# Products of ones on the tensor engine before x arrives, a power in two halves, and another order of work in the first block of an attention and feed-forward kernel

## The reference

```python
xn = _layernorm(x, axis=-1)
x = x + attn(xn, qkv_w, qkv_norm_w, proj_w, proj_norm_w, norm_w, s) + ffn(xn, w_gate, w_up, w_down)
# attn: h = rmsnorm(xn) * qkv_norm_w; q, k, v = h @ ternary(qkv_w).T, 16 heads of 32
#       per chunk of 128 tokens: (q k^T * decay mask) v + (q * decay) S, with a running state S
#       two rmsnorms of the result, then @ ternary(proj_w).T
# ffn:  (silu(xn @ w_gate.T) * (xn @ w_up.T)) @ w_down.T, 2048 hidden features
# ternary(w): w over its mean absolute value, rounded and clipped to -1, 0, 1
```

## Time and profile before

| | |
|---|---|
| median of 3 runs | 1362.63 us (1362.43 to 1362.7) |
| the profiled execution's own time | 1361.45 us |
| its span | 1359.7 us |
| granted TensorE clock, mean of the span | 1.000 |
| busy: PE, DVE, ACT, POOL | 98%, 68%, 36%, 5% of the span |

### The profile page before, as it was taken

One profiled execution on the slowest core, in us unless ns is written; L12 is line 12 of the kernel. 1 busy time (PEld: TensorE's weight loads), 2 busy tenths in 40 slices (PEclk: granted clock), 3 DMA queues, 4 the chain that ended last, 5 costly groups with the idle time before them and its releaser, 6 DMA issues.

```text
span 1359.7 us, 21928 instructions
## 1 busy us (share of the span) xinstructions
PE 1334.2 (98%) x8332; PEld 721.3 (53%) x8332; DVE 924.6 (68%) x1886; ACT 486.5 (36%) x915; POOL 67.5 (5%) x88
## 2 busy tenths in 40 slices
PE   5899999999999999999999999999999999999999
PEld 3455555555455554555545555555545555455554
DVE  6988995576655766657766677657775576755655
ACT  7964633233233332333323233223332233232331
POOL 5600000000000000000000000000000000000000
DMA  8242234113431145211351113510145112431121
GB/s 314 83 142 67 87 73 120 26 32 67 111 88 28 30 79 124 53 32 40 71 140 35 29 40 70 148 40 26 38 85 132 32 30 49 94 94 32 32 48 47
DMA packets 193767, 98.72 MB, mean 73 GB/s; under 512 B 127104, under 2 KB 179328, under 8 KB 192000
## 3 DMA queue, kind: packets, MB, share of 16 engines
q1 hardware_dynamic: 193376, 97.30, 28.3%
q10 hardware_dynamic: 288, 0.01, 0.0%
HBM read 34.35 MB, written 8.39 MB: 31 GB/s over the span
## 4 chain that ended last, share of the span: by engine, by line
PE 94%; DVE 3%; ACT 1%; DMA 1%; SPq 1%; issue 1%; POOL 0%; DVEq 0%; POOLq 0%
PE bank L517 89%; PE bank L559 2%; PE bank L586 1%; PE bank L588 1%; DVE wg_lo L1292 0%; SPq L935 0%; DMA xin<-x 0%; ACT wg_lo L1142 0%; DMA k_stack<-k_parts 0%; DVE arena L861 0%; DMA q_stack<-q_parts 0%; DVE arena L747 0%; DVE xt L748 0%; DVE wd_lo L1292 0%; DVE wu_lo L1292 0%
## 5 line engine op out<-in xcount | busy, mean ns | idle before, releaser
L517 PE MATMUL bank<-wd_hi,arena 128*128 128x512 f16 x1024 | 317.0, 379 | 0.0
L517 PE MATMUL bank<-xt,wg_hi 128*128 128x512 f16 x1024 | 306.5, 381 | 3.6 <-ACT ql L728 1.6
L517 PE MATMUL bank<-xt,wu_hi 128*128 128x512 f16 x1024 | 304.6, 379 | 0.0
L517 PE MATMUL bank<-xt,wg_lo 128*128 128x512 f16 x512 | 195.0, 381 | 0.0
L517 PE MATMUL bank<-wd_lo,arena 128*128 128x512 f16 x512 | 194.0, 379 | 0.0
L517 PE MATMUL bank<-xt,wu_lo 128*128 128x512 f16 x512 | 194.0, 379 | 0.0
L517 PEld LDWEIGHTS bank<-wd_hi,arena 128*128 128x128 f16 x1024 | 100.2, 98 | 115.3
L789 DVE TENSOR_TENSOR sm<-bank,mask 128x512 f32<-128x512 f32 x128 | 88.1, 688 | 105.4 <-PE bank L559 105.3
L517 PEld LDWEIGHTS bank<-xt,wu_hi 128*128 128x128 f16 x1024 | 99.0, 98 | 104.4 <-issue 0.5
L517 PEld LDWEIGHTS bank<-xt,wg_hi 128*128 128x128 f16 x1024 | 98.2, 98 | 103.5 <-issue 4.6
L673 ACT ACTIVATE sm_hi<-sm 128x512 f16<-128x512 f32 x128 | 80.1, 626 | 193.5 <-DVE sm L789 193.5
(11 more groups left out here) (200 smaller groups left out, 1492.2 us busy)
## 6 DMA issues: line engine op xcount, KB each, us to landing
k_stack<-k_parts SPq DMA_DIRECT2D x192, 64.0 KB, 2.2
q_stack<-q_parts SPq DMA_DIRECT2D x192, 64.0 KB, 2.2
arena<-x SPq DMA_DIRECT2D x8, 1024.0 KB, 5.9
out<-arena SPq DMA_DIRECT2D x32, 256.0 KB, 2.4
xin<-x SPq DMA_DIRECT2D x30, 256.0 KB, 4.5
stage<-up_t SPq DMA_DIRECT2D x4, 1024.0 KB, 5.3
stage<-down_t SPq DMA_DIRECT2D x4, 1024.0 KB, 4.9
stage<-gate_t SPq DMA_DIRECT2D x3, 1024.0 KB, 4.8
```

Of the source, the lines that this page charges most:

```text
L517: last = e.matmul(dst, a, b, start=start and n == 0, stop=stop and n == len(lhs) - 1)
```

## The change

On the PE, ahead of the first list, come 30 products of 128x128 by 128x512, written to the bank of SC, which nothing else uses then; they read the part of the transposed x that is filled later, set to ones by one DVE memset. Eight follow that memset, four follow the arrival of each of the four tiles of x, and six follow the first half of the variances. Nothing reads their result.

DVE announces the variance for the layer norm (var_0 part 0) as soon as it is written and that for the rms norm (part 1) later; POOL takes the power of each with an instruction of its own, where it took one over both. HX waits for the second.

The order lists of the first block are new for all engines. Every item is still there. Only the changed lines of the lists' beginnings and ends are shown.

```diff
@@ FIRST_ORDER: the lists of the first block, to where it needs Q, K and V, and their ends @@
     "PE": [
-        ('WT', 0), ('FX', 0), ('FX', 1), ('FX', 2), ('FX', 3), ('WT', 1), ('G', 0), ('U', 0), ('G', 1), ('U', 1), ('G', 2),
-        ('SO', 0), ('FT', 0), ('WT', 2), ('FT', 1), ('WT', 3), ('U', 2), ('G', 3), ('U', 3), ('FT', 2), ('G', 4), ('SO', 1),
-        ('U', 4), ('G', 5), ('WT', 4), ('FT', 3), ('U', 5), ('WT', 5), ('G', 6), ('U', 6), ('K', 0), ('Q', 0), ('V', 0),
-        ('V', 1), ('SC', 0, 0), ('KT', 0), ('G', 7), ('O', 0, 0), ('OX', 0, 0), ('SC', 0, 1), ('Q', 1), ('K', 1), ('KV', 0),
...
-        ('SC', 7, 1), ('G', 15), ('OX', 7, 0), ('KV', 7), ('O', 7, 1), ('U', 15), ('OX', 7, 1), ('D', 2, 2), ('D', 2, 3),
-        ('D', 3, 0), ('D', 3, 1), ('D', 3, 2), ('ZT', 2), ('ZT', 3), ('D', 3, 3), ('PJ', 2), ('PJ', 3),
+        ('WT', 0), ('FX', 0), ('FX', 1), ('FX', 2), ('FX', 3), ('WT', 1), ('G', 0), ('U', 0), ('G', 1), ('WT', 2), ('U', 1),
+        ('G', 2), ('U', 2), ('WT', 3), ('FT', 0), ('FT', 1), ('FT', 2), ('G', 3), ('U', 3), ('G', 4), ('SO', 0), ('WT', 4),
+        ('U', 4), ('G', 5), ('U', 5), ('G', 6), ('SO', 1), ('WT', 5), ('U', 6), ('FT', 3), ('K', 0), ('Q', 0), ('V', 0),
+        ('V', 1), ('G', 7), ('SC', 0, 0), ('KT', 0), ('D', 0, 0), ('O', 0, 0), ('OX', 0, 0), ('SC', 0, 1), ('K', 1),
...
+        ('SC', 7, 1), ('G', 15), ('U', 15), ('OX', 7, 0), ('KV', 7), ('O', 7, 1), ('PJ', 1), ('OX', 7, 1), ('D', 2, 2),
+        ('D', 2, 3), ('D', 3, 0), ('D', 3, 1), ('ZT', 2), ('ZT', 3), ('D', 3, 2), ('D', 3, 3), ('PJ', 2), ('PJ', 3),
...
     "ACT": [
-        ('WA', 0), ('WA', 1), ('WH', 0, 0), ('FX', 0), ('FX', 1), ('FX', 2), ('FX', 3), ('SA', 0), ('SA', 1), ('SA', 2),
-        ('WH', 0, 1), ('WH', 0, 2), ('WH', 1, 0), ('WH', 0, 3), ('WH', 1, 1), ('G', 0), ('SA', 3), ('WH', 1, 2), ('SA', 4),
-        ('WH', 1, 3), ('UH', 0), ('SA', 5), ('G', 1), ('WA', 2), ('WA', 3), ('UH', 1), ('FT', 0), ('G', 2), ('WH', 2, 0),
-        ('WH', 2, 1), ('WH', 3, 0), ('WH', 3, 1), ('FT', 1), ('G', 3), ('SA', 6), ('UH', 2), ('UH', 3), ('FT', 2), ('WA', 4),
-        ('G', 4), ('EL', 0), ('EM', 0), ('WA', 5), ('G', 5), ('UH', 4), ('UM', 0), ('UM', 1), ('UM', 2), ('UM', 3),
-        ('UM', 4), ('UM', 5), ('UH', 5), ('FT', 3), ('K', 0), ('G', 6), ('Q', 0), ('WH', 4, 0), ('WH', 4, 1), ('WH', 5, 0),
-        ('WH', 5, 1), ('V', 0), ('V', 1), ('UH', 6), ('SC', 0, 0), ('KT', 0), ('UM', 6), ('Q', 1), ('SC', 0, 1), ('K', 1),
...
+        ('WA', 0), ('WA', 1), ('FX', 0), ('WH', 0, 0), ('FX', 1), ('FX', 2), ('FX', 3), ('WH', 0, 1), ('WH', 0, 2),
+        ('WA', 2), ('WH', 1, 0), ('WH', 0, 3), ('WH', 1, 1), ('G', 0), ('WH', 1, 2), ('SA', 0), ('SA', 1), ('SA', 2),
+        ('G', 1), ('UH', 0), ('SA', 3), ('SA', 4), ('SA', 5), ('WA', 3), ('WH', 1, 3), ('G', 2), ('WH', 2, 0), ('UH', 1),
+        ('SA', 6), ('G', 3), ('WH', 2, 1), ('WH', 3, 0), ('FT', 0), ('FT', 1), ('UH', 2), ('UH', 3), ('WA', 4), ('WH', 3, 1),
+        ('G', 4), ('FT', 2), ('EL', 0), ('EM', 0), ('G', 5), ('WA', 5), ('UM', 0), ('UM', 1), ('UM', 2), ('UM', 3),
+        ('UM', 4), ('UM', 5), ('FT', 3), ('UH', 4), ('UH', 5), ('K', 0), ('G', 6), ('Q', 0), ('WH', 4, 0), ('WH', 4, 1),
+        ('WH', 5, 0), ('V', 0), ('UH', 6), ('WH', 5, 1), ('V', 1), ('SC', 0, 0), ('KT', 0), ('UM', 6), ('K', 1),
...
     "DVE": [
         ('S4', 0), ('N4', 0), ('WT', 0), ('WC', 0, 0), ('FX', 0), ('FX', 1), ('FX', 2), ('FX', 3), ('WT', 1), ('WC', 0, 1),
-        ('WC', 1, 0), ('WC', 1, 1), ('WC', 0, 2), ('WC', 0, 3), ('U', 0), ('QN', 0), ('HX', 0), ('WC', 1, 2), ('WC', 1, 3),
-        ('UL', 0), ('SS', 0), ('U', 1), ('HX', 1), ('HX', 2), ('HX', 3), ('SO', 0), ('WT', 2), ('WT', 3), ('FT', 0),
-        ('UL', 1), ('U', 2), ('WC', 2, 0), ('WC', 2, 1), ('WC', 3, 0), ('FT', 1), ('U', 3), ('WC', 3, 1), ('UL', 2),
-        ('UL', 3), ('RD', 0), ('SO', 1), ('FT', 2), ('U', 4), ('RD', 1), ('WT', 4), ('U', 5), ('HD', 0), ('WT', 5),
-        ('UL', 4), ('WN', 0), ('UL', 5), ('FT', 3), ('K', 0), ('U', 6), ('Q', 0), ('WC', 4, 0), ('WC', 4, 1), ('WC', 5, 0),
-        ('SC', 0, 0), ('V', 0), ('WC', 5, 1), ('SL', 0, 0), ('KT', 0), ('V', 1), ('SC', 0, 1), ('Q', 1), ('SL', 0, 1),
...
+        ('WC', 1, 0), ('WC', 1, 1), ('WC', 0, 2), ('QN', 0), ('WC', 0, 3), ('U', 0), ('WC', 1, 2), ('HX', 0), ('HX', 1),
+        ('HX', 2), ('HX', 3), ('WT', 2), ('U', 1), ('UL', 0), ('WT', 3), ('SS', 0), ('U', 2), ('WC', 1, 3), ('UL', 1),
+        ('WC', 2, 0), ('U', 3), ('WC', 2, 1), ('WC', 3, 0), ('FT', 0), ('SO', 0), ('FT', 1), ('UL', 2), ('WC', 3, 1),
+        ('FT', 2), ('UL', 3), ('U', 4), ('RD', 0), ('RD', 1), ('U', 5), ('WT', 4), ('SO', 1), ('HD', 0), ('WT', 5),
+        ('WN', 0), ('FT', 3), ('UL', 4), ('UL', 5), ('K', 0), ('U', 6), ('Q', 0), ('WC', 4, 0), ('WC', 4, 1), ('WC', 5, 0),
+        ('V', 0), ('SC', 0, 0), ('WC', 5, 1), ('SL', 0, 0), ('KT', 0), ('V', 1), ('D', 0, 0), ('SC', 0, 1), ('KV', 0),
...
+        ('D', 2, 2), ('NA', 3), ('D', 2, 3), ('NR', 1), ('ST', 1), ('NZ', 1), ('D', 3, 0), ('XN', 1), ('D', 3, 1), ('TX', 2),
+        ('TX', 3), ('TH', 2), ('ZT', 2), ('D', 3, 2), ('ZT', 3), ('D', 3, 3), ('TH', 3), ('PJ', 2), ('PJ', 3),
...
     "POOL": [
-        ('S4', 0), ('RD', 2), ('RD', 3), ('RD', 4), ('RD', 5), ('RD', 6), ('MS', 0), ('NR', 0), ('ST', 0), ('NR', 1),
+        ('S4', 0), ('RD', 2), ('RD', 3), ('RD', 4), ('MS', 0), ('RD', 5), ('RD', 6), ('NR', 0), ('ST', 0), ('NR', 1),
         ('ST', 1),
...
     "SP": [
-        ('WL', 3), ('WL', 4), ('WL', 5), ('YL', 0), ('K', 0), ('Q', 0), ('WL', 6), ('WL', 7), ('V', 0), ('Q', 1), ('K', 1),
-        ('Q', 2), ('K', 2), ('WL', 8), ('Q', 3), ('K', 3), ('Q', 4), ('K', 4), ('Q', 5), ('K', 5), ('WL', 9), ('WL', 10),
-        ('K', 6), ('Q', 6), ('WL', 11), ('Q', 7), ('K', 7), ('TH', 0), ('TH', 1), ('XT', 0), ('TX', 2), ('TX', 3), ('TH', 2),
+        ('WL', 3), ('WL', 4), ('WL', 5), ('YL', 0), ('K', 0), ('Q', 0), ('WL', 6), ('WL', 7), ('V', 0), ('K', 1), ('Q', 1),
+        ('Q', 2), ('K', 2), ('WL', 8), ('K', 3), ('Q', 3), ('Q', 4), ('K', 4), ('WL', 9), ('WL', 10), ('Q', 5), ('K', 5),
+        ('WL', 11), ('K', 6), ('Q', 6), ('K', 7), ('Q', 7), ('TH', 0), ('TH', 1), ('XT', 0), ('TX', 2), ('TX', 3), ('TH', 2),
@@ -398,6 +399,7 @@
         "pro_chain", "beta_sum", "ternary", "piece_max", "piece_scale",
         "beta_total", "beta_part", "clipped"))
     s_inverse, s_clip_pool, s_total = sem("beta_inverse"), sem("clipped_pool"), sem("beta_read")
+    s_warm = sem("warm_tile")
     s_spread, s_allmax = sem("piece_max_spread"), sem("piece_max_read")
     s_var0, s_rs0 = sem("first_variance"), sem("first_scale")
     s_whi, s_wlo = ([sem(f"piece_{k}{n}") for n in range(2)] for k in ("hi", "lo"))
@@ -1067,9 +1069,9 @@
             def first_item(it):
                 kind, n = it[:2]
                 if kind == "S4":
-                    e.wait_ge(s_var0, 1)
-                    e.tensor_tensor(rs_0, var_0[:, 0:2, :], mhalf_0.rearrange("p (a c) -> p a c", a=2), ALU.pow)\
-                        .then_inc(s_rs0, 1)
+                    for k in range(2):
+                        e.wait_ge(s_var0, k + 1)
+                        e.tensor_tensor(rs_0[:, k, :], var_0[:, k, :], mhalf_0[:, 0:TPB], ALU.pow).then_inc(s_rs0, 1)
                     for j in range(GROUPS):
                         e.tensor_scalar(lam_q[:, j, :], ramp, part[:, 0, j:j + 1], part[:, 1, j:j + 1], ALU.mult, ALU.add)
                         last = e.tensor_scalar(lam_k[:, j, :], ramp_back, part[:, 0, j:j + 1], part[:, 2, j:j + 1],
@@ -1151,6 +1153,19 @@
         @block.tensor
         def _(e):
             e.sem_inc(pe["ZT"].sem, pe["ZT"].before)
+            e.wait_ge(s_warm, 1)
+
+            def keep_busy(n):
+
+                for _ in range(n):
+                    e.matmul(b_sc[:, :], xt[0][:, 0, 0:P], xt[0][:, 0, :], start=True, stop=True)
+
+            keep_busy(8)
+            for c in range(TPB):
+                e.wait_ge(ld_first[c], 16)
+                keep_busy(4)
+            e.wait_ge(s_var0, 1)
+            keep_busy(6)
             e.wait_ge(s_ident, 3)
             def first_item(it):
                 kind, n = it
@@ -1190,6 +1205,7 @@
                 ins.then_inc(s_pro, 1)
                 e.wait_ge(s_pro, done[0])
 
+            e.memset(xt[0][:, 0, :], 1.0).then_inc(s_warm, 1)
             e.memset(state1[:, :], 1.0)
             e.wait_ge(s_ident, 3)
             link(e.tensor_reduce(pm4[:, :], ident[:, :].rearrange("p (d h) -> p h d", h=HPG), axis=AX.X, op=ALU.add))
@@ -1214,7 +1230,8 @@
                     for c in range(TPB):
                         last = e.bn_aggr(mv_0[:, c, :], st6_0[:, c, :])
                     link(last)
-                    link(e.tensor_scalar(var_0[:, 0, :], mv_0[:, :, 1], LN_EPS, None, ALU.add))
+                    e.tensor_scalar(var_0[:, 0, :], mv_0[:, :, 1], LN_EPS, None, ALU.add).then_inc(s_var0, 1)
+                    e.wait_ge(s_var0, 1)
                     link(e.reciprocal(var_0[:, 2, :], var_0[:, 0, :]))
```

(1 more changed line is left out.)

## The result

The changed kernel takes 1366.13 us, the median of 8 runs (1365.6 to 1367.95), beside 1362.51 for the kernel before (8 runs, 1361.9 to 1362.94): ratio 1.0029, 95% interval 1.0018 to 1.004. It is 3.6 us slower, just outside the predicted range. Its profiled execution took 1365.87 us with a span of 1364.1, 4.4 us more than the span before. Busy shares are as they were (PE 98%, DVE 68%); the mean granted clock is 0.996 where it was 1.000.

The account below looks back on a forecast made before the run. Three engines together were taken to limit the first block to about 80 us, the PE everything from about 85. Losses of 8.2 us against 8.8 made 0.6 less, median 1362.63 to 1362.0, range 1357.0 to 1366.0.

Parts of the forecast that it names:

- Rival 3: At the first G: the clock has fallen again and the products are in vain, 1363.0 us; chance 0.18.
- the wait for QN: First block: DVE's U(0) stands behind QN, whose transfer lands at 25.0 us; PE waits 1.3 us at U(1).
- the sum: PE idle time in the new order, added from 19 to 80 us: 7.8 us, and 0.2 for the start.
- the sum's end at 80 us: At O(0,0), 77.7 to 79.4 us with D(0,0) already done: PE between 0.8 us ahead and 0.9 behind.
- Does the clock hold?: Nearly idle 4.9 us ahead of G(0): a fallen clock costs 2.5 us, 1.5 hidden, 1363.0 instead of 1362.0; left undecided.
- Rival 2: POOL's MS ahead of RD(5) delays K(0), decided by K(0) past 64.5: 3.4 us more, 1365.4, or 1366.3; chance 0.23.
- Rival 1: The new order closes the waits at WT(4), G(6), U(6), K(0) and O(0,0): 4.5 us less, 1357.5; chance 0.36.

Follow-up runs that it names:

- after_bridge: The changed kernel with 33 more products of 256 columns in the PE's gap ahead of the first G: 1365.6 us, 1.0018 to the kernel before.
- fix1: The changed kernel with SO(0) put back early on PE and DVE, POOL's order still new: 1364.26 us, 1.0012 to the kernel before.
- hyb_old_mspool: Old order up to K(0), new behind it, products and halved power, with POOL's MS ahead of RD(5) and RD(6): 1364.29 us, 1.0008 to the kernel before.
- after_pool2: The changed kernel with WN behind V(1), POOL's RD(5) ahead of MS, and HD behind UL(5) on DVE: 1366.1 us, 1.0026 to the kernel before.
- fix4: The changed kernel with SO(0) and SO(1) early and POOL's old order, RD(5) and RD(6) ahead of MS: 1365.97 us, 1.002 to the kernel before.
- after_again: The changed kernel unaltered, run and profiled a second time beside the two mixed orders: 1366.67 us, 1.0025 to the kernel before.
- o_only: The changed kernel without the products of ones and with one power, so the new order alone: 1367.25 us, 1.0037 to the kernel before.

## Why the prediction was wrong

**Right.** The products (at 424 ns from 1.5 us, at the fast pace from 5.26, done at 10.3), the power in halves (normalization at 9.95; nothing bought: 0.9994), G(0) at 18.71 (19.0), QN at 25.00, POOL's first RD at 47.12 (about 47), RD(4) done at 56.1 (54 to 56), though MS ended at 62.2 for my 61.5 at most, K(0) at 65.73 (63.2 to 66.5, taken at 64). Rival 3's mechanism came in part: the first G lost its pace, U(1) started at 28.38 with a G of 4.3 us and at 29.41 with one of 5.1 (forecast 28.25 and 29.3), and with a G of 2.9 us, in `after_bridge`, it started no earlier, so part of the slow G is hidden in the wait for QN.

**Luck.** The PE's idle time from 18 to 80 us is 7.6 us, forecast 8.0, but not where I had it: the waits of 1.3 us at U(1) and 1.2 at U(6) didn't come, K(0)'s was 2.65 for my 1.8, and 0.7 us lie ahead of G(0), where the sum hadn't begun.

**The step that failed** is the sum's end at 80 us: "so the PE stands between 0.8 us ahead and 0.9 behind", and then "Behind that DVE has slack (18.59 of 20 us busy in its fullest stretch shown); I take 0.2 us for PJ(2)". DVE wrote Q(0)'s lo part at 72.95, beyond the 70.5 to 72.4; WN beside RD(6) was in no term (+3.3 us on two instructions). The first O came at 80.33, beyond 79.4, which is 4.4 us later than before or 1.8 behind after D(0,0)'s 2.6; and behind it the PE stood idle for 3.4 us more (2.7 of it at 80 to 100) for my 0.2. That the late start is what costs is shown by the crossed halves: 4.8 us with the new start, a gain of 1.65 with the new rest behind the old one. That WN's 3.3 us carry it isn't: `after_wn` moved WN behind the attention's start, K(0)'s lo part came 1.9 us earlier, and the time was the same. SO(0), late at 47 us and in the sum only through POOL and K(0), carries about half of the loss (`fix1`); what carries the rest is open. The transfers that stack K and Q ahead of SC(2,0), from one place in SBUF to another, I hadn't walked through: 2.04 us, one of the waits of over 1 us between 90 and 200 us that I had taken for none. And "From about 85 us on the PE is never waited for" isn't so of the kernel before: the rows above show 1.3 us at 200 to 240.

**The second one** is "Does the clock hold?", asked for G(0) alone. It fell at K(0) and at 100 us as well, behind waits of 2.65 and 2.04 us, 1.7 and 1.8 us: a PE that comes to work that isn't ready can pay twice. Together 16.3 of idle and clock stands against my 8.2; before, 11.4 against my 8.8, since I had left out 0.8 at the start, 0.5 at 80 to 100 and 1.3 at block 1. The errors of 8.1 and 2.6 us differ by 5.5; the profiled execution missed 1360.85 by 5.0.

**The rivals.** Rival 2 named POOL's order, and with the old start that order alone costs 4.3 us, forecast 3.4 to 4.3, but its decision point (K(0) later than 64.5) was the wrong meter: in `hyb_old_mspool` K(0) starts at 64.37. With the new start it explains no part of the loss: RD(5) taken back ahead of MS gains nothing (`after_pool2`), nor does POOL's whole old order with the sums early (`fix4`). Rival 1 is true of the half I gave least thought: the rest of the lists does close gaps, 1.65 us, when the start isn't late.

## What to carry to other kernels

Cut a new order at a point that all engines pass and run each half with the other's old half: two crossed runs, beside one with the old order throughout, found a gain of 1.65 us inside a change that lost 3.6. Before an instruction stream is reordered, list which operations of DVE will run beside GpSimd's, not only which engine waits for which. And count PE idle and clock loss together: filling the one can merely move the time to the other. And where one early item can run at either pace from one execution to the next, as the first G here, look at its length before two profiles are compared.

## What the runs showed of the hardware

**Contention of DVE and GpSimd.** Beside a GpSimd operation on SBUF, DVE's operations from SBUF to SBUF are longer by nearly what is left of it (1.6 to 1.7 us for 1.8 in these three): 128x512 in 2.11 us (0.49 alone), 128x512 of two SBUF inputs in 2.37 (0.68), 128x1024 in 2.38 (0.69). These three end 0.3 to 0.6 us behind the GpSimd operation that they began beside, of 2.46, 1.94 and 2.35 us. The addition with a PSUM bank as input at 50.66, beside GpSimd's operation of 49.76 to 51.7, kept its 0.68. The Trainium skill (SBUF — State Buffer, SBUF: two separate sides) says that the shared pair of ports is "an **exclusive lock**, not a bandwidth split"; the traces agree.

**The clock.** After 22 products at the fast pace up to 10.3 us, the transposes up to 14.2 and then two products of one column in 4.5 us, the first G began fast, and the granted clock stood at 0.50 from 20 to 22 us. Fast pace at an item's start says nothing of its end. The Trainium skill (TensorE: Matmul & The Clock Gate, Part 1) has the throttled clock as the default to which an idle PE falls back; the trace agrees. In `after_again` the same G, behind the same products, was slow from its first product, 5.10 us for the twelve. Where it falls isn't fixed: that second profile of the changed kernel has no fall at K(0), behind a wait of 2.66 us (clock sum 4.9, idle 12.7, its losses at the start and at 100 us), and `o_only` has none there nor behind the 2.04 us ahead of SC(2,0). The paces read here are those of two levels, 1.2 and 2.4 GHz: 424 and 216 ns for 512 columns.

**Two powers.** GpSimd's power of 128x4 takes 1.05 us (two in 2.11) and of 128x8 1.67: halving the columns doesn't halve it.
